# Edge counting in groups of 13 targets with keys fetched from device memory, and a re-ordered start, in a one-core graph layer

## The chip, the cores and the metric

The kernel runs on one core of a Trainium2 chip. The core has five engines with a queue each: TensorE (matmul; its weight loads are listed apart), VectorE, ScalarE, GpSimd and SyncE (which here only issues DMAs). They meet through semaphores, and 16 DMA engines serve all queues. The metric is the device time of one execution in microseconds, the median of the timed runs.

## The reference

One layer of a graph transformer over N = 1250 nodes with D = 1024 features, and 41250 edges (20000 random ones in both directions and a self loop for each node), sorted by target `dst`:

```python
xn = _layernorm(x)
# graph convolution: adds self loops once more, symmetric norm
deg  = segment_sum(ones, dst);  dinv = rsqrt(deg)
gnn  = relu(segment_sum((xn @ W)[src] * (dinv[src] * dinv[dst])[:, None], dst) + b)
# linear attention, 16 heads: phi(k) = elu(k) + 1
mix  = (phi(Q) @ (phi(K).T @ V)) / (phi(Q) @ sum(phi(K)) + 1e-6) @ Wo.T + bo
x = x + gnn + mix
# gated feed-forward with two gelu layers of 512, then back to 1024
x = x + ffn(_layernorm(x))
```

The message sum is done as a product with the 1250 x 1250 matrix of edge counts, so the kernel must count how many edges go from each source to each target.

## The kernel before, in words

Nodes are tiled by 128: NT = 10 tiles, the last of 98. Every float32 product is made of three float32r matmuls with high and low parts, so each weight slice of 128 x 512 needs a copy ("hi", `weight_hi`) and a remainder ("lo", `weight_lo`) before use. Remainders are made strictly in order of the slices, since each waits for the count `w_ready` of the one before; the list `LO_FIRST` says which of the first ten VectorE makes, GpSimd makes the others.

The first phase has 40 steps: 4 slabs of key and value weights by 10 node tiles. In a step TensorE makes 24 matmuls of 512 columns (`gemm_rows`), then the key-value sums of the step before (`kv_sum`). In steps 1 to 8 it first transposes the next node tile (`transpose_tile`), in step 0 the second tile within the product. A node tile goes this way: rows arrive in `xrow` (two buffers), VectorE takes the statistics (`ln_stats`), ScalarE the root (`ln_root`), VectorE finishes (`ln_finish`), ScalarE applies (`ln_apply`), TensorE transposes, ScalarE copies the high part (`transposed_hi`), VectorE makes the remainder (`transposed_lo`). VectorE takes the statistics of tile s + 3 in its step s, behind its work on the unit of that step (`kb`, `kmin`).

Edges are counted in the same steps. VectorE prepares keys, constants and chunk ranges in `edge_parts` of its steps 1 to 5 and 8, with an all-reduce on GpSimd between. A group ("window") is 16 targets of a tile. SyncE loads the group's first chunk number from `bounds` and copies 6 chunks of 128 keys from the key table in SBUF (`keys_load`); VectorE makes one-hots of sources and of (target, source tile) (`window`); TensorE multiplies them, 6 matmuls of 160 columns a group; ScalarE copies the counts out (`adj_out`); VectorE adds a finished tile up (`count_tile`). From step 10 on there are three groups a step, `windows_of`; TensorE does the groups of a step behind its product in the next step, two ahead of `kv_sum` and the rest behind. A group with more than 6 chunks would take a slower path under an `If`, which these inputs never enter.

Then follow queries, the graph product, its aggregation, the mixing and the feed-forward part, which the change does not touch. Engines are in-order queues and everything is placed by hand: what stands behind a wait on its engine waits too.

## Time and profile before

| | us |
|---|---|
| median of 3 runs (lowest to highest) | 1010.98 (1010.98 to 1013.32) |
| the profiled execution | 1012.45 |
| its span between first and last instruction | 1010.6 |
| TensorE busy | 986.4 (98%) |
| VectorE busy | 560.3 (55%) |
| ScalarE busy | 292.6 (29%) |
| GpSimd busy | 143.2 (14%) |
| mean granted clock of TensorE | 0.996 of 2.4 GHz |

The profiled execution lies between the lowest and the highest of the timed runs. Busy time of TensorE includes matmuls that overlap their neighbours, so costs are read as distances between starts. "L1444" is a line of the printed kernel.

### The profile page before, as it was taken

How to read it: one execution, taken by the hardware profiler on the slowest of the kernel's cores; microseconds unless marked ns; L12 is line 12 of the kernel's file. 1: busy time of each engine (PE TensorE's matmuls, PEld its weight loads, DVE VectorE, ACT ScalarE, POOL GpSimd, SP SyncE). 2: the span in 40 equal slices, each digit the busy share in tenths (PEclk: the TensorE clock that was granted, in tenths of full speed). 3: DMA queues.
4: the chain of work that ended last, by engine and by line, in shares of the span. 5: the costliest groups of instructions: out<-in, count | busy, mean ns of one | idle time of the engine just before them, and what ended most of it. 6: DMA issues, size and time to landing. Idle time of an engine off the chain costs nothing.

```text
span 1010.6 us, 13193 instructions
## 1 busy us (share of the span) xinstructions
PE 986.4 (98%) x4932; PEld 835.3 (83%) x4932; DVE 560.3 (55%) x1033; ACT 292.6 (29%) x564; POOL 143.2 (14%) x192
## 2 busy tenths in 40 slices
PE   4999999999999999999999999999999999999998
PEld 3878888888889988978787688767778999999986
DVE  5886768778754788893112465446655412122354
ACT  5783213214114243241212222113213212135300
POOL 7011001001002023050300000000300203055100
PEclk9999999999999999999999999999999999999999
DMA  7313103013002003122020566445421402010053
GB/s 279 116 50 97 30 17 111 18 32 98 15 28 85 26 26 134 50 70 93 21 86 15 161 190 190 139 146 167 162 88 54 167 1 84 1 42 1 21 186 138
DMA packets 44077, 86.74 MB, mean 86 GB/s; under 512 B 16152, under 2 KB 20612, under 8 KB 43992
## 3 DMA queue, kind: packets, MB, share of 16 engines
q1 hardware_dynamic: 35512, 57.20, 17.3%
q0 software_dynamic: 8480, 28.45, 8.8%
q8 instruction: 48, 0.79, 0.3%
q14 instruction: 37, 0.30, 0.1%
HBM read 61.38 MB, written 23.76 MB: 84 GB/s over the span
## 4 chain that ended last, share of the span: by engine, by line
PE 90%; DVE 6%; ACT 1%; issue 1%; POOL 1%; DMA 1%; DVEq 0%; ACTq 0%; POOLq 0%
PE PS L1405 10%; PE PS L1407 10%; PE PS L1406 10%; PE PS L1511 9%; PE PS L1512 9%; PE PS L1513 9%; PE PS L1569 5%; PE PS L1571 4%; PE PS L1444 3%; PE PS L1588 3%; PE PS L1589 3%; PE PS L1590 3%; PE PS L1640 2%; PE PS L1642 2%; PE PS L1641 2%; PE PS L1420 2%
## 5 line engine op out<-in xcount | busy, mean ns | idle before, releaser
L1405 PE MATMUL PS<-ring,act_t 128*128 128x512 f32 (+1 forms) x480 | 194.6, 405 | 1.7 <-DVE act_t L967 0.9
L1407 PE MATMUL PS<-ring,act_t 128*128 128x512 f32 (+1 forms) x480 | 190.7, 397 | 0.0
L1406 PE MATMUL PS<-ring,act_t 128*128 128x512 f32 (+1 forms) x480 | 190.2, 396 | 0.0
L1511 PE MATMUL PS<-act_t,ring 128*128 128x416 f32 (+1 forms) x432 | 159.3, 369 | 1.4 <-POOL ring L423 1.3
L1512 PE MATMUL PS<-act_t,ring 128*128 128x416 f32 (+1 forms) x432 | 152.1, 352 | 0.0
L1513 PE MATMUL PS<-act_t,ring 128*128 128x416 f32 (+1 forms) x432 | 151.8, 351 | 0.0
L1405 PEld LDWEIGHTS PS<-ring,act_t 128*128 128x128 f32 (+1 forms) x480 | 89.9, 187 | 23.9 <-POOL ring L423 1.6
L1407 PEld LDWEIGHTS PS<-ring,act_t 128*128 128x128 f32 (+1 forms) x480 | 89.5, 186 | 22.4
L1406 PEld LDWEIGHTS PS<-ring,act_t 128*128 128x128 f32 (+1 forms) x480 | 89.8, 187 | 21.4 <-issue 0.5
L1511 PEld LDWEIGHTS PS<-act_t,ring 128*128 128x128 f32 x432 | 81.3, 188 | 6.8 <-issue 3.4
L1512 PEld LDWEIGHTS PS<-act_t,ring 128*128 128x128 f32 x432 | 81.4, 188 | 4.1 <-issue 3.4
L1513 PEld LDWEIGHTS PS<-act_t,ring 128*128 128x128 f32 x432 | 81.2, 188 | 0.9
L1190 DVE RECIPROCAL rec<-rec 128x416 f32<-128x416 f32 (+1 forms) x24 | 65.9, 2746 | 0.0
L722 ACT ACTIVATE ctile<-PS 128x160 uint16<-128x160 f32 x80 | 23.2, 300 | 137.2 <-PE PS L1444 136.3
L604 POOL DMA_DIRECT2D stage_x<-in_wslices_dram x54 | 29.3, 547 | 207.5 <-DVE ring L423 203.7
L1056 DVE TENSOR_TENSOR oh_dst<-iota,kcur 128x960 bf16<-128x960 int16 x80 | 52.0, 650 | 0.0
L1340 DVE SCALAR_TENSOR_TENSOR hb<-PS,scl,sil 128x416 f32<-128x416 f32 (+1 forms) x12 | 7.8, 651 | 75.3 <-PE PS L1513 75.3
L1125 DVE TENSOR_TENSOR kb<-PS,kvb 128x256 f32<-128x256 f32 (+1 forms) x40 | 16.9, 424 | 52.6 <-issue 38.3
L423 POOL TENSOR_TENSOR ring<-stage,ring 128x512 fp32r<-128x512 f32 x23 | 31.0, 1348 | 99.9 <-ACT ring L728 97.7
L1055 DVE TENSOR_TENSOR oh_src<-iota,kcur 128x768 bf16<-128x768 int16 x80 | 44.1, 551 | 0.3
L423 POOL TENSOR_TENSOR ring<-stage_x,ring 128x512 fp32r<-128x512 f32 x28 | 38.2, 1364 | 38.0 <-ACT ring L728 26.9
L1444 PE MATMUL PS<-oh_dst,oh_src 128*128 128x160 bf16 x480 | 43.2, 233 | 0.0
(185 smaller groups left out, 1654.1 us busy)
## 6 DMA issues: line engine op xcount, KB each, us to landing
stage_x<-in_wslices_dram POOLq DMA_DIRECT2D x54, 256.0 KB, 4.2
stage<-in_wslices_dram POOLq DMA_DIRECT2D x42, 256.0 KB, 3.6
xr<-x_d SPq DMA_DIRECT2D x18, 512.0 KB, 3.4
phin_d<-phiq SPq DMA_DIRECT2D x8, 625.0 KB, 3.2
xrow<-in_x_dram SPq DMA_DIRECT2D x9, 512.0 KB, 3.7
xh<-in_x_dram SPq DMA_DIRECT2D x18, 256.0 KB
x_d<-xh SPq DMA_DIRECT2D x18, 256.0 KB
x_d<-xr SPq DMA_DIRECT2D x9, 512.0 KB, 2.7
```

What stands on the lines that cost most here:

```text
L423: eng.tensor_tensor(ring[:, slot(k), 1, :], stage_buf(n), ring[:, slot(k), 0, :].bitcast(F32), ALU.subtract).then_inc(w_ready, 1)
L1055: dve.tensor_tensor(oh_src[:, b], count(P), pairs(kcur[:, dt % 2, j, 0], P), ALU.is_equal)
L1056: dve.tensor_tensor(oh_dst[:, b], count(WCOLS), pairs(kcur[:, dt % 2, j, 1], WCOLS), ALU.is_equal).then_inc(onehot, 1)
L1190: dve.reciprocal(rec[:, i % 2, 0:n], rec[:, i % 2, 0:n]).then_inc(rec_ready, 1)
L1405: pe.matmul(out_ap, node_rows(0, k, t), ring[:, slot(k0 + k), 0, :], start=(k == 0), stop=False)
L1406: pe.matmul(out_ap, node_rows(1, k, t), ring[:, slot(k0 + k), 0, :], start=False, stop=False)
L1407: ins = pe.matmul(out_ap, node_rows(0, k, t), ring[:, slot(k0 + k), 1, :], start=False, stop=(k == KD - 1))
L1444: ins = pe.matmul(PS[:, b, 0:WCOLS], oh_src[:, o, j // 2, :, j % 2], oh_dst[:, o, j // 2, :, j % 2], start=(j == 0), stop=(j == STATIC_CHU ...
L1511: pe.matmul(out_ap, w[0], x_t[:, 0, k, o:o + n], start=(k == 0), stop=False)
L1512: pe.matmul(out_ap, w[0], x_t[:, 1, k, o:o + n], start=False, stop=False)
L1513: ins = pe.matmul(out_ap, w[1], x_t[:, 0, k, o:o + n], start=False, stop=(k == nk - 1))
L1569: pe.matmul(out_ap, lhs, h_rows(half, 0, st), start=(st == 0), stop=False)
```

## The change

It groups 13 targets (the last group of a tile has 11) in place of 16, 10 groups a tile and 100 in all, with 4 chunks of 128 edges each. The edges are laid out by rows (328 consecutive edges a partition) in place of columns. The key table is stored to device memory (`keys_d`), and each group's 512 keys are fetched from there, starting at any edge and not only at a multiple of 128. The first edge of every group is found by comparing with row bounds and by four small matmuls in TensorE's steps 4 and 6; GpSimd's all-reduce is gone. The fallback now counts all edges for a tile if any group has more than 512 edges or the edges are unsorted. There are four groups a step in steps 10 to 34, and five one-hot buffers in place of three.

At the start the first tile's rows come in two halves of 512 columns with a semaphore each, and the first norm is applied in halves ahead of all weight copies. VectorE makes the remainders of slices 0, 1, 3, 5 and 7, with the third tile's statistics ahead of the last. The root and finish of the third tile stand ahead of step 0. The third tile's rows go to `st_blk` (a buffer used much later) and are requested when the fourth weight slice is in, ahead of the edges; GpSimd clears `st_blk` afterwards. The second tile's transposes stand two slices later in the first product.

```diff
@@ constants @@
-STATIC_CHUNKS = 6
+STATIC_CHUNKS = 4
+CAPACITY = STATIC_CHUNKS * P
-OH_BUFS = 3
+OH_BUFS = 5
-WIN = 16
+WIN = 13
-LO_FIRST = (3, 5, 7)
+LO_FIRST = (0, 1, 3, 5, 7)
@@ windows_of @@
-    if 10 <= step < 37:
-        return list(range(3 * (step - 10), min(3 * (step - 9), NWIN)))
+    if 10 <= step < 35:
+        return list(range(4 * (step - 10), 4 * (step - 9)))
@@ block.sync @@
-            sp.dma_start(xrow[:, 0, :], xrows(x, 0)).then_inc(x_in[0], 16)
-            sp.dma_start(xrow[:, 1, :], xrows(x, 1)).then_inc(x_in[1], 16)
-            sp.dma_start(e_src[:], src_cols).then_inc(edges_in, 16)
-            sp.dma_start(e_dst[:], dst_cols).then_inc(edges_in, 16)
-            sp.dma_start(d_rows[0:ROWS_P], dst_rows).then_inc(edges_in, 16)
+            for g in range(2):
+                sp.dma_start(xrow[:, 0, 512 * g:512 * g + 512], x[0:P, 512 * g:512 * g + 512]).then_inc(x_first[g], 16)
+            sp.dma_start(x_tile(1), xrows(x, 1)).then_inc(x_in[1], 16)
+            sp.wait_ge(stage_in[stage_slot(3)], 16)
+            sp.dma_start(x_tile(2), xrows(x, 2)).then_inc(x_in[2], 16)
+            sp.dma_start(e_src[:], src_rows).then_inc(edges_in, 16)
+            sp.dma_start(e_dst[:], dst_rows).then_inc(edges_in, 16)
...
-            for t in range(2, NT):
-                sp.wait_ge(xn_ready, t - 1)
-                sp.dma_start(xrow[0:rows(t), t % 2, :], xrows(x, t)).then_inc(x_in[t % 2], 16)
+            for t in range(3, NT):
+                sp.wait_ge(xn_ready, t - 1 if t > 4 else t - 2)
+                sp.dma_start(x_tile(t), xrows(x, t)).then_inc(x_in[x_buf(t)], 16)
+                if t == 3:
+                    sp.wait_ge(keys_ready, 1)
+                    sp.dma_start(keys_d.rearrange("(p c) k -> p (c k)", p=P),
+                                 keys[:, 0:ROWL].rearrange("p c k -> p (c k)")).then_inc(keys_stored, 16)
...
-                    first = sp.value_load(bounds[0:1, w:w + 1], min_val=0, max_val=NCH)
-                    sp.dma_start(kraw[:, dt % KEY_BUFS, j], keys[:, bass.ds(first, STATIC_CHUNKS), :]).then_inc(keys_got[dt], 16)
+                    first = sp.value_load(bounds[0:1, w:w + 1], min_val=0, max_val=LAST_FIRST)
+                    sp.dma_start(kraw[:, dt % KEY_BUFS, j],
+                                 keys_d[bass.ds(first, CAPACITY), :].rearrange("(p c) k -> p c k", p=P)).then_inc(keys_got[dt], 16)
@@ block.gpsimd @@
-            pool.wait_ge(score_ready, 1)
-            nc.gpsimd.partition_all_reduce(sall[:], smax[:], P, RMAX).then_inc(bounds_max, 1)
+            pool.wait_ge(xn_ready, 3)
+            nc.gpsimd.memset(st_blk[:], 0.0).then_inc(consts, 1)
@@ block.vector @@
-            def edge_ranges():
...
+            def edge_rows():
+
+                link(dve.tensor_copy(d_row[:, 0:ROWL + 1], e_dst[:]))
+                link(dve.tensor_copy(first_d[:], d_row[:, 0:1]))
+                link(dve.memset(first_d[0:1], -1.0))
+                link(dve.tensor_scalar(row_of[:], thr[:], first_d[:], None, ALU.is_gt))
+                dve.scalar_tensor_tensor(row_of[:], thr[:], d_row[:, ROWL:ROWL + 1], row_of[:], ALU.is_le,
+                                         ALU.mult).then_inc(rows_known, 1)
+
+            def edge_order():
+                link(dve.tensor_tensor(below[:], d_row[:, 0:ROWL], d_row[:, 1:ROWL + 1], ALU.is_gt))
+                link(dve.tensor_reduce(unsorted[:], below[:], AX.X, ALU.max))
...
+            edge_parts = {1: edge_keys, 2: edge_constants, 3: edge_rows, 4: edge_order, 5: edge_starts, 7: edge_bounds}
@@ block.tensor @@
-                    ins = pe.matmul(PS[:, b, 0:WCOLS], oh_src[:, o, j // 2, :, j % 2], oh_dst[:, o, j // 2, :, j % 2],
+                    n = width(w) * NT
+                    ins = pe.matmul(PS[:, b, 0:n], oh_src[:, o, j // 2, :, j % 2], oh_dst[:, o, j // 2, 0:n, j % 2],
...
+            def group_rows():
+                a = slice(0, NWIN + 1)
+                pe.wait_ge(rows_known, 1)
+                pe.matmul(PS[a, 7, 0:ROW_COLS], row_of[:], d_row[:], start=True, stop=True)
+                pe.matmul(PS[a, 7, THR_COL:THR_COL + 1], thr[0:1], ones[0:1, 0:1], start=True, stop=True).then_inc(rows_got, 1)
```

Three places show how instructions moved. The first is SyncE's queue at its beginning, before: rows of node tiles go to `xrow`, those of tiles 2 to 9 by the eight loads of L445; `d_rows` are the targets for the ranges.

```order
L434 DMA xrow<-in_x_dram 128x1024
L435 DMA xrow<-in_x_dram 128x1024
L436 DMA e_src<-in_src_cols_dram 128x336
L437 DMA e_dst<-in_dst_cols_dram 128x336
L438 DMA d_rows<-in_dst_rows_dram 108x384
L440 DMA kvb<-in_bkv_dram 128x512 x2
L441 DMA bq_sb<-in_bq_dram 128x8
L442 DMA scl<-in_scales_dram 128x16
L445 DMA xrow<-in_x_dram 128x1024 x7
```

And with the change, where `st_blk` holds the third tile's rows and `keys_d` is the key table in device memory:

```order
L464 DMA xrow<-in_x_dram 128x512 x2
L465 DMA xrow<-in_x_dram 128x1024
L467 DMA st_blk<-in_x_dram 128x1024
L468 DMA e_src<-in_src_rows_dram 128x328
L469 DMA e_dst<-in_dst_rows_dram 128x329
L471 DMA kvb<-in_bkv_dram 128x512 x2
L472 DMA bq_sb<-in_bq_dram 128x8
L473 DMA scl<-in_scales_dram 128x16
L476 DMA xrow<-in_x_dram 128x1024
L479 DMA keys_d<-keys 128x656
L476 DMA xrow<-in_x_dram 128x1024 x5
```

The third tile moved ahead of the edges, and the store of the keys stands between the loads of the fourth and the fifth tile.

The second is ScalarE from its first root to the tenth weight copy, before (`ring` is written by weight copies, `xn` by the norm, `act_t` by the high part of a transposed tile, `ln` by the root):

```order
L690 ACTIVATE ln<-ln 128x1
L728 ACTIVATE ring<-stage 128x512 x2
L704 ACTIVATE xn<-xrow,ln 128x1024
L728 ACTIVATE ring<-stage 128x512 x2
L711 ACTIVATE act_t<-PS 128x4x128 x2
L690 ACTIVATE ln<-ln 128x1
L728 ACTIVATE ring<-stage_x 128x512 x2
L704 ACTIVATE xn<-xrow,ln 128x1024
L728 ACTIVATE ring<-stage_x 128x512 x4
```

And with the change:

```order
L724 ACTIVATE ln<-ln 128x1
L739 ACTIVATE xn<-xrow,ln 128x512
L742 ACTIVATE xn<-xrow,ln 128x512
L767 ACTIVATE ring<-stage 128x512
L724 ACTIVATE ln<-ln 128x1
L749 ACTIVATE act_t<-PS 128x4x128 x2
L767 ACTIVATE ring<-stage 128x512 x3
L767 ACTIVATE ring<-stage_x 128x512
L742 ACTIVATE xn<-xrow,ln 128x1024
L767 ACTIVATE ring<-stage_x 128x512 x5
L724 ACTIVATE ln<-ln 128x1
L749 ACTIVATE act_t<-PS 128x4x128 x2
```

The norm of the first tile stands in halves ahead of the copies, two of the roots stand ahead of the step loop's work, and each tile's high part comes earlier among the copies.

The third is TensorE in a counting step, from the end of its product to the branch of the fallback, before:

```order
L1406 MATMUL PS<-ring,act_t 128x512
L1407 MATMUL PS<-ring,act_t 128x512
L1405 MATMUL PS<-ring,act_t 128x512
L1406 MATMUL PS<-ring,act_t 128x512
L1407 MATMUL PS<-ring,act_t 128x512
L1444 MATMUL PS<-oh_dst,oh_src 128x160 x12
L1420 MATMUL PS<-phik,vt 128x128 x2
L1444 MATMUL PS<-oh_dst,oh_src 128x160 x6
L1450 COMPARE_AND_BRANCH
```

And with the change:

```order
L1441 MATMUL PS<-ring,act_t 128x512
L1439 MATMUL PS<-ring,act_t 128x512
L1440 MATMUL PS<-ring,act_t 128x512
L1441 MATMUL PS<-ring,act_t 128x512
L1479 MATMUL PS<-oh_dst,oh_src 128x130 x8
L1454 MATMUL PS<-phik,vt 128x128 x2
L1479 MATMUL PS<-oh_dst,oh_src 128x130 x8
L1485 COMPARE_AND_BRANCH
```

Eighteen matmuls of 160 columns became sixteen of 130, four groups in two pairs around the key-value sums.

## Rows read from the trace of the kernel before

**Rows 1.** The page: span, then busy us, share and instructions of each engine

```profile
span 1010.6 us, 13193 instructions
...
PE 986.4 (98%) x4932; PEld 835.3 (83%) x4932; DVE 560.3 (55%) x1033; ACT 292.6 (29%) x564; POOL 143.2 (14%) x192
```

**Rows 2.** Waits of TensorE: who waited, for whom, us in total, times, longest

```profile
PE PS L1387 <- ACT xn L704: 16.2, 5, 9.5
```

**Rows 3.** Timeline: start us, us, engine line op out<-in xcount [idle before]

```profile
4.45 1.42 DVE L937 BATCH_NORM_STATS2 stats<-xrow 128x6 f32<-128x512 f32 x2 [4.45 <-DMA xrow<-in_x_dram]
...
8.15 1.23 ACT L704 ACTIVATE xn<-xrow,ln 128x1024 f32<-128x1024 f32 x1
...
9.52 1.94 PE L1387 MATMUL PS<-ident,xn 128*128 128x128 f32 x8 [9.52 <-ACT xn L704]
...
16.48 1.29 POOL L423 TENSOR_TENSOR ring<-stage_x,ring 128x512 fp32r<-128x512 f32 x1 [1.52 <-ACT ring L728]
...
17.88 0.69 DVE L423 TENSOR_TENSOR ring<-stage_x,ring 128x512 fp32r<-128x512 f32 x1 [2.12 <-POOL ring L423]
...
22.62 1.24 ACT L704 ACTIVATE xn<-xrow,ln 128x1024 f32<-128x1024 f32 x1 [2.06 <-DVE ln L960]
...
23.92 1.97 PE L1387 MATMUL PS<-ident,xn 128*128 128x128 f32 x8 [2.84 <-ACT xn L704]
```

**Rows 4.** The timeline of VectorE in its steps 1 to 4

```profile
30.84 0.51 DVE L979 SCALAR_TENSOR_TENSOR keys<-e_dst,e_hi 128x336 f32<-128x336 int32 x1
...
32.78 1.42 DVE L937 BATCH_NORM_STATS2 stats<-xrow 128x6 f32<-128x512 f32 x2
...
36.53 1.28 DVE L967 TENSOR_TENSOR act_t<-PS,act_t 128x512 fp32r<-128x512 f32 x2
...
45.02 0.19 DVE L992 MEMSET smax<- 128x160 f32 x1
...
47.93 0.42 DVE L1125 TENSOR_TENSOR kb<-PS,kvb 128x256 f32<-128x256 f32 x1
...
53.56 0.27 DVE L1006 TENSOR_SCALAR score<-thr,d_rng 108x80 f32<-108x80 f32 x1
...
56.18 0.42 DVE L1125 TENSOR_TENSOR kb<-PS,kvb 128x256 f32<-128x256 f32 x1
```

**Rows 5.** The timeline of TensorE, the transposes of three steps

```profile
32.29 1.04 PE L1387 MATMUL PS<-ident,xn 128*128 128x128 f32 x8
...
39.19 1.04 PE L1387 MATMUL PS<-ident,xn 128*128 128x128 f32 x8
...
68.99 1.04 PE L1387 MATMUL PS<-ident,xn 128*128 128x128 f32 x8
```

**Rows 6.** The timeline of TensorE, starts of two steps without counting

```profile
82.52 0.47 PE L1405 MATMUL PS<-ring,act_t 128*98 128x512 f32 x1
...
88.52 0.48 PE L1405 MATMUL PS<-ring,act_t 128*128 128x512 f32 x1
```

**Rows 7.** The timeline of TensorE, a step with counting

```profile
122.85 1.03 PE L1444 MATMUL PS<-oh_dst,oh_src 128*128 128x160 bf16 x12
123.72 0.65 PE L1420 MATMUL PS<-phik,vt 128*128 128x128 f32 x4
124.20 0.59 PE L1444 MATMUL PS<-oh_dst,oh_src 128*128 128x160 bf16 x6
...
130.25 1.03 PE L1444 MATMUL PS<-oh_dst,oh_src 128*128 128x160 bf16 x12
```

**Rows 8.** SyncE: the key loads in its timeline, and the row loads of L445

```profile
81.30 37.61 SPq L464 DMA_DIRECT2D kraw<-keys  x32
...
DMA to landing us min/median/max: 3.5/4.7/7.5
```

**Rows 9.** TensorE near 699 us: timeline, and a stretch with granted clock (PEclk)

```profile
699.37 0.90 PE L1387 MATMUL PS<-ident,xn 128*128 128x128 f32 x3 [2.02 <-ACT xn L704]
...
699.50:702.70 3.20, 3.20 (x12) 2.91 (x13) 2.91 (x7) 1.04 (x4) 0.00 (x0) 0.50 0.59 191
```

283 lines of the change are left out of this document (150 added, 133 removed).

## Prediction, made before the changed kernel had run

> **What bounds the kernel now.** I read the page first. TensorE is busy for 986.4 of 1010.6 us [rows 1], so what counts is the work on TensorE itself and the few places where it stands still. The waits of TensorE name one large item: transposes that wait for a normalised tile from ScalarE, 16.2 us in five waits, the longest 9.5 us [rows 2]. One of them, 2.02 us, ends at 699.37 us [rows 9]; the others lie in the first 62 us. So a change can gain in two ways: fewer matmul columns after 62 us, where TensorE hardly waits, and less standing still before.
>
> In the counting steps the timeline of TensorE shows what counting costs. A step without it takes 88.52 - 82.52 = 6.00 us [rows 6], one with three groups 130.25 - 122.85 = 7.40 us [rows 7]. The 18 matmuls of 160 columns cost 1.40 us a step: 12 of them take 123.72 - 122.85 = 0.87 us, 72.5 ns each, and 0.095 us is change-over. Nothing waits there, so what leaves these steps leaves the total.
>
> Before 62 us the chain is another. TensorE starts at 9.52 us behind statistics (4.45) and the application of the norm (8.15), and gets its third tile only at 23.92 us [rows 3]. After that VectorE sets the pace, since it carries the preparation of the edges beside the norms [rows 4]: a step with transposes takes TensorE 39.19 - 32.29 = 6.90 us when nothing waits, but the next four take 68.99 - 39.19 = 29.80 us [rows 5], 2.2 us more than four of these. From 68.99 us on TensorE is bound by itself.
>
> **Counting: 13 targets and 4 chunks.** Before, 80 groups by 6 matmuls of 160 columns: 26 steps by 1.40 plus a rest of two groups, 12 x 0.0725 = 0.87 us, 37.3 us in all. Now 100 groups by 4 matmuls, 16 in each of 25 steps, 130 columns each (110 in the last group of every tile). The price of a 130-column matmul is not in the trace. From above it is bounded by today's 72.5 ns; from below by taking 30 columns off at the slope of the large matmuls: 24 of 512 columns take the 6.00 us of a bare step [rows 6] less 124.20 - 123.72 = 0.48 us of key-value sums [rows 7], 230 ns each, so (230 - 72.5)/352 = 0.45 ns a column and 59.0 ns. One column a cycle at 2.4 GHz, the level granted here, takes off 12.5 ns and gives 60.0. I take 59.5 ns, near the lower end, since 160 columns already take little more than their own 66.7 ns. A step then pays 16 x 0.0595 + 0.095 = 1.05 us, 25 steps 26.2 us, less 0.3 us for the narrow groups: 25.9 to 26.0 us. **Counting saves 11.3 us** (5.9 us at the upper price).
>
> The Trainium skill (TensorE: Matmul & The Clock Gate, section Back-to-back issue gap) speaks against this: it gives some 81 ns for every pair of weight load and 128-column matmul in a sustained stream. This trace, with 72.5 ns for 160 columns, is already below it; by the page's figure 400 matmuls would cost 32.4 us and change-over, a gain of 2.5 us in place of 11.3.
>
> VectorE builds fewer elements for it: per step four pairs of one-hots with 512 and 520 elements against three with 768 and 960, so its load falls along with the step, and I cost it at nothing; TensorE's long step hides it. ScalarE copies out four results a step in place of three, two of them ahead of the exponential; each fits under the key-value sums that follow on TensorE. SyncE fetches the keys with one load a group, 1.2 us each by its timeline (37.61 us for 32) [rows 8]. The first ten must be there for VectorE's step 10 near 94 us. The boundaries, now without GpSimd's all-reduce and one step earlier, come near 75 us, so the fetch of the first tile is done near 89 us: hidden by 5 us. The largest group of these sorted inputs holds 486 edges against a capacity of 512, so the fallback path is not entered.
>
> **The start.** The first rows come in halves, so one of the two statistics (half of 1.42 us) runs before 4.45 us and the norm is ready 0.7 us sooner. The application now goes ahead of the weight copies and in halves, and the first transposes move from 9.52 to about 7.8 us. That alone gives little: the first unit still waits for its slices, whose remainders alternate between VectorE (0.69 us) and GpSimd (1.29 us) and whose eighth ends at 17.88 + 0.69 = 18.57 us [rows 3]. In the new order the first transposed tile reaches VectorE near 9.7 us, its remainder is done at 11.0 and that of the second slice at 11.7; three turns of GpSimd and two of VectorE later it is 17.0, the third tile's statistics run until 17.75, and the eighth remainder ends near 18.4. What helps is that statistics and root of the third tile now stand ahead of this eighth slice and its finish right behind, where before 1.9 us of statistics and 1.3 us of another tile's remainder lay between. With some 1.2 us for the finish (five short instructions) and 1.3 us for the application, the third tile's transposes move from 23.92 to about 20.95 us, **3.0 us sooner**, and VectorE's step 1 with them: the edge keys are ready at 28.35 in place of 30.84 + 0.51 = 31.35 us [rows 4].
>
> **A new wait takes this back.** SyncE's queue now holds, between the rows of the fourth and the fifth tile, the store of the key table, and this waits for the edge keys. The fifth tile's rows are thus asked for at 28.35 + 0.45 us (0.45 for issuing the store). Such a load takes 3.5 us at least [rows 8]; behind a store of 336 KB up to 0.9 us more. They land between 32.3 and 33.2 us, and VectorE's statistics of this tile, which follow the edge keys within a microsecond and began at 32.78 us before [rows 4], begin there. Behind them on VectorE stand the step's key sums, the next norm and the next remainder. So VectorE's step 2 begins between 0.5 us earlier and 0.4 us later than before, though all ahead of it is 3 us earlier.
>
> From there the side work shrinks: the ranges of step 3, 47.93 - 45.02 = 2.91 us, become five short instructions of 1.4 us, and the scores of step 4, 56.18 - 53.56 = 2.62 us, become two over 328 columns, 1.1 us (an instruction of 336 columns takes 0.51 us) [rows 4]. VectorE's steps are then about 7.1 us at most and no longer hold TensorE. The fifth tile's transposes start behind the chain that those statistics open: 36.53 - 32.78 = 3.75 us to the next remainder [rows 4] and 1.3 us for this, so at 37.85 us; four steps of 6.9 us follow, plus the new row matmul of 330 columns (330/128 x 0.24 = 0.62 us, where two of 128 columns take 0.48 us [rows 7]), one of 101 columns (0.19) and two of one column (0.2 each at most, by the same row): 66.6 to 66.9 us at the place that the trace of before has at 68.99 us [rows 5]. **The start gains 2.2 us** (1.8 to 2.8). From here TensorE is its own bound in both.
>
> **Sum.** The profiled execution took 1012.45 us, 1.85 more than its span. Minus 11.3 and 2.2 it is 998.95. Two of three timed runs gave 1010.98, 1.47 below the profiled one; on the median the forecast is 1010.98 - 13.5 = 997.5 us. The half-speed stretch at 699.5 us (clock 0.50 for 3.4 us behind a stand of 2 us [rows 9]) costs 1.7 us when it comes, and may come or stay away in either kernel; this is the width of the forecast, 995.5 to 999.5.
>
> **Rivals.**
> The pace of short matmuls does not follow their columns. For it: a weight load accompanies each. Against: 160 columns are near their column time. At 72.5 ns the gain is 5.9 + 2.2: 1002.9 us.
> The weight loads do not hide under shorter matmuls, and a pair costs more than today. Counting gains nothing when 400 matmuls and 2.4 us of change-over reach 37.3 us, at 87 ns; midway from 72.5, at 80 ns, it gains 37.3 - 32.0 - 2.4 = 2.9 us: 1010.98 - 2.9 - 2.2 = 1005.9 us. Against it: nothing in the counting step of before shows a load that sticks out. The page of the Trainium skill named above describes this case.
> The fifth tile's rows aren't late after all, for instance because the edge keys come much sooner than I count. Then the 3.0 us carry through and the shorter side work adds its own: transposes of the eighth tile near 63.7 us, a gain of 5.3, and 994.4 us.
> The fifth tile's rows are later still (the store takes its full 2 to 3 us ahead of them): the start gains nothing, 999.7 us and up to 1001.
> Slower: fetching keys from device memory in 32-byte pieces runs at another pace than 1.2 us a load. With up to 1.7 us nothing waits; with p us a load counting ends near 75 + 100 p + 5 us against 269 without waits, so from p = 2.03 it eats the whole gain, and at twice today's pace, 2.4 us, it gives 997.5 + 51 = 1048 us. Against it: the trace shows SyncE's own instructions filling the 1.2 us, not the transfer.
>
> **Chances.** Forecast as summed 0.62; short matmuls at today's price 0.12; start gain carried through 0.10; start gains nothing 0.08; weight loads that stick out 0.03; slow fetches or another wait in counting that makes it slower 0.05 (0.01 of it near no change). The range 994 to 1003 us holds the first, second and fourth and half of the third. A difference under 0.3% (3 us) can't be told from none. All cases but the last lie 5 us or more below the median: faster 0.94, within 0.3% 0.02, slower 0.04.
>
> **What would show it.** Counting: steps near 7.05 us from the twelfth on, twelve to sixteen matmuls with starts 58 to 61 ns apart, no idle time of TensorE ahead of them. Start: first transposes at 7.8 us, the third tile's near 21. The new wait: VectorE's statistics of the fifth tile idle for 3 to 4 us behind the load of rows, the place named as DMA. The transposes of the eighth tile near 66.8 us. I am wrong if VectorE doesn't wait there, if the counting matmuls stay above 70 ns apart, or if one-hot building waits for keys.

## The result, and the profile after

| | before | changed |
|---|---|---|
| median of 6 runs each, us | 1012.67 | 1007.33 |
| lowest to highest | 1010.98 to 1016.65 | 1004.61 to 1007.82 |
| profiled execution | 1012.45 | 1007.65 |
| its span | 1010.6 | 1005.8 |
| TensorE busy | 986.4 | 980.2 |

The ratio is 0.9938, with a 95% interval of 0.9916 to 0.9961. The kernel is faster by 5.3 us in the medians (6.3 by the ratio); 13.5 us were forecast, and 1007.33 lies outside the range of 994 to 1003 us. (Of the 9.8 us between 997.5 and 1007.33, 1.7 are the median of before, which was 1010.98 when the forecast was made; 8.1 are the change.) The forecast calls the place at 68.99 us "the eighth tile"; counted from the first, these are the ninth tile's transposes, and so they are called here.

The page of the changed kernel, its lines that answer to [rows 1]:

```profile
span 1005.8 us, 13325 instructions
...
PE 980.2 (97%) x4860; PEld 827.2 (82%) x4860; DVE 545.5 (54%) x1069; ACT 293.9 (29%) x585; POOL 139.8 (14%) x189
```

TensorE's waits in it (who, for whom, us in total, times, longest) answer to [rows 2]:

```profile
PE PS L1421 <- ACT xn L739: 8.2, 1, 8.2
PE PS L1421 <- ACT xn L742: 5.6, 3, 2.2
PE PS L1439 <- DVE act_t L1004: 2.6, 1, 2.6
PE PS L1454 <- DVE phik L1170: 1.8, 1, 1.8
```

The 16.2 us of before are now 13.8 on the two lines of the norm, but 2.6 and 1.8 us stand beside them (the one for `act_t` was 0.9 us before), and one wait is new: that for `phik`. It stands in the middle of the start, as TensorE's timeline shows, to be held against [rows 3, 5]:

```profile
8.20 1.94 PE L1421 MATMUL PS<-ident,xn 128*128 128x128 f32 x8 [8.20 <-ACT xn L739]
...
23.20 0.97 PE L1421 MATMUL PS<-ident,xn 128*128 128x128 f32 x7 [1.39 <-ACT xn L742]
...
30.40 1.08 PE L1421 MATMUL PS<-ident,xn 128*128 128x128 f32 x8
...
38.86 0.71 PE L1454 MATMUL PS<-phik,vt 128*128 128x128 f32 x4 [1.81 <-DVE phik L1170]
41.80 1.96 PE L1421 MATMUL PS<-ident,xn 128*128 128x128 f32 x8 [2.22 <-ACT xn L742]
```

(The line at 23.20 us is cut off by its window; all eight transposes take 1.08 us.) Up to the fourth tile (30.40 us, 32.29 before) the change leads by 1.9 us. Part of that is clock: before, TensorE runs at half its clock from 23.56 us on for 3.4 us, which [rows 3, 5] show in eight transposes that take 1.97 us at 23.92 and 1.04 us later; with the change it doesn't there. The fifth tile's transposes start at 41.80, where before they start at 39.19. Behind them TensorE runs at half its clock (columns: stretch, length, then busy us of TensorE, weight loads, VectorE, ScalarE and GpSimd, the granted clock, DMA share, GB/s):

```profile
40.50:47.30 6.80, 5.50 (x17) 4.76 (x18) 6.28 (x20) 5.67 (x8) 0.00 (x0) 0.51 0.25 77
```

The place that [rows 5] have at 68.99 us comes at 73.55 us. So the start loses 4.6 us. It was forecast to gain 2.2. From the first counting matmul to the first product of the queries it is 208.8 us before (100.65 to 309.48) and 199.6 now (105.22 to 304.79): 9.3 us gained. Behind that the two kernels take the same (701 us). 9.3 - 4.6 = 4.7, against 4.8 between the spans: nothing is left to explain elsewhere.

The chain that ended last names what made the fifth tile late (start us, us, what):

```profile
31.26 0.51 DVE keys L1016
31.79 0.34 SPq L479
32.13 0.04 issue
32.17 4.42 DMA xrow<-in_x_dram
36.62 0.71 DVE stats L974
...
40.24 0.23 DVE ln L997
40.49 1.25 ACT xn L742
41.74 0.06 issue
41.80 1.96 PE PS L1421 x8
```

Edge keys, then SyncE's store of them (L479), then the load that stands behind it in SyncE's queue, then the statistics, norm and transposes: the new wait of the forecast, in its place. VectorE idles for it:

```profile
36.62 1.42 DVE L974 BATCH_NORM_STATS2 stats<-xrow 128x6 f32<-128x512 f32 x2 [4.08 <-DMA xrow<-in_x_dram]
```

### The profile page after: what moved, and what is told of

Its sections match the earlier page's. It is cut to its first block, busy times and chain, and to the rows that moved or that the text cites. A ratio compares the mean times of both kernels' runs of the same rounds, so it can differ in the third digit from the quotient of the medians.

```text
span 1005.8 us, 13325 instructions
## 1 busy us (share of the span) xinstructions
PE 980.2 (97%) x4860; PEld 827.2 (82%) x4860; DVE 545.5 (54%) x1069; ACT 293.9 (29%) x585; POOL 139.8 (14%) x189
## 4 chain that ended last, share of the span: by engine, by line
PE 91%; DVE 5%; DMA 1%; ACT 1%; issue 1%; POOL 1%; SPq 0%; DVEq 0%; ACTq 0%; POOLq 0%
PE PS L1439 11%; PE PS L1441 10%; PE PS L1440 10%; PE PS L1561 9%; PE PS L1560 9%; PE PS L1562 9%; PE PS L1618 5%; PE PS L1620 4%; PE PS L1638 3%; PE PS L1639 3%; PE PS L1637 3%; PE PS L1479 2%; PE PS L1454 2%; PE PS L1691 2%; PE PS L1690 2%; PE PS L1689 2%
## 5 line engine op out<-in xcount | busy, mean ns | idle before, releaser
L761 ACT ACTIVATE ctile<-PS 128x130 uint16<-128x130 f32 x100 | 23.7, 283 | 115.0 <-PE PS L1479 115.0
L640 POOL DMA_DIRECT2D stage<-in_wslices_dram x42 | 23.0, 550 | 182.5 <-DVE ring L440 179.9
L440 POOL TENSOR_TENSOR ring<-stage,ring 128x512 fp32r<-128x512 f32 x21 | 28.5, 1355 | 106.2 <-ACT ring L767 104.4
L1086 DVE TENSOR_TENSOR oh_dst<-iota,kcur 128x520 bf16<-128x520 int16 x100 | 42.2, 422 | 0.0
L1085 DVE TENSOR_TENSOR oh_src<-iota,kcur 128x512 bf16<-128x512 int16 x100 | 41.9, 419 | 0.3
```

The lines of the kernel that those rows point to most:

```text
L440: eng.tensor_tensor(ring[:, slot(k), 1, :], stage_buf(n), ring[:, slot(k), 0, :].bitcast(F32), ALU.subtract).then_inc(w_ready, 1)
L640: pool.dma_start(stage_buf(n), wslices[n]).then_inc(stage_in[stage_slot(n)], 16)
L1085: dve.tensor_tensor(oh_src[:, b], count(P), pairs(kcur[:, dt % 2, j, 0], P), ALU.is_equal)
L1086: dve.tensor_tensor(oh_dst[:, b], count(WCOLS), pairs(kcur[:, dt % 2, j, 1], WCOLS), ALU.is_equal).then_inc(onehot, 1)
```

## The experiments

All times are medians; "ratio" is to the kernel before on the same chip, with its 95% interval. The last two columns are the starts of the fifth and ninth tile's transposes in the profiled execution. e1 to e4 ran side by side, so did e5 to e8, e9 to e12, and e13 with e14; medians compare best within such a group.

| kernel | us | ratio | 5th | 9th |
|---|---|---|---|---|
| before | 1012.67 | | 39.19 | 68.99 |
| changed | 1007.33 | 0.9938 [0.9916, 0.9961] | 41.80 | 73.55 |
| e10, changed again | 1007.01 | 0.9943 [0.9931, 0.9956] | 41.41 | 72.12 |
| e1, store behind the rows | 998.76 | 0.9864 [0.9836, 0.9892] | 37.35 | 66.81 |
| e12, e1 again | 1000.41 | 0.9878 [0.9863, 0.9893] | 37.45 | 66.91 |
| e4, before with the store | 1016.62 | 1.0038 [1.0024, 1.0053] | 41.78 | 72.88 |
| e9, changed, stands filled | 1005.74 | 0.9934 [0.9922, 0.9947] | 42.22 | 71.67 |
| e8, old start, new counting | 1003.31 | 0.9906 [0.9886, 0.9926] | 40.33 | 69.41 |
| e2, e1 and late slices | 998.66 | 0.9866 [0.9838, 0.9895] | 36.71 | 65.95 |
| e3, e1 and whole first rows | 999.53 | 0.9871 [0.9843, 0.9900] | 36.60 | 66.06 |
| e7, e1, e2 and e3 | 998.49 | 0.9862 [0.9841, 0.9883] | 35.77 | 65.23 |
| e11, e7 with the store in place | 1003.91 | 0.9916 [0.9902, 0.9931] | 39.49 | 70.20 |
| e13, e2 and late clearing | 999.16 | 0.9864 [0.9839, 0.9889] | 37.22 | 66.31 |
| e14, e7 and late clearing | 999.07 | 0.9859 [0.9836, 0.9882] | 35.61 | 64.92 |
| e5, e1 without the fallback | 999.60 | 0.9871 [0.9849, 0.9892] | 35.52 | 64.98 |
| e6, e1 with half the columns | 994.37 | 0.9818 [0.9798, 0.9838] | 36.67 | 66.12 |

### Is it the place of the store? e1, e4, e10, e12

e1 moves the store behind all row loads:

```diff
             for t in range(3, NT):
                 sp.wait_ge(xn_ready, t - 1 if t > 4 else t - 2)
                 sp.dma_start(x_tile(t), xrows(x, t)).then_inc(x_in[x_buf(t)], 16)
-                if t == 3:
-                    sp.wait_ge(keys_ready, 1)
-                    sp.dma_start(keys_d.rearrange(...), keys[...]).then_inc(keys_stored, 16)
+            sp.wait_ge(keys_ready, 1)
+            sp.dma_start(keys_d.rearrange(...), keys[...]).then_inc(keys_stored, 16)
```

> One edit to the changed kernel: the store of the key table leaves its place between the row loads of the fourth and the fifth tile and stands behind all row loads. Theory A (the store's wait for the edge keys delays the fifth tile's rows, and the stand of TensorE that follows brings the half-speed stretch at 40.5 us): VectorE's wait of 4.1 us at 36.6 us is gone, the fifth tile's transposes (41.80 us in the changed kernel) start at 37.5 to 38, no half-speed stretch follows them, the ninth... tile of transposes that stood at 73.55 us starts at 66 to 67.5, and the median falls from 1007.3 to about 1000.5 us. Rival B (VectorE's own steps of 7.1 us set the pace anyway): the wait goes, but only some 3 us come back, about 1004 us. Rival C (the rows are late for another reason): no change.

e4 is the reverse: the kernel before, with a store of its key table ahead of the fifth tile's load. Its only other addition is a wait for this store ahead of the key loads, which start at 85.6 us, long after it.

```diff
             for t in range(2, NT):
                 sp.wait_ge(xn_ready, t - 1)
+                if t == 4:
+                    sp.wait_ge(keys_ready, 1)
+                    sp.dma_start(keys_d, keys[:].rearrange("p c k -> p (c k)")).then_inc(keys_stored, 16)
                 sp.dma_start(xrow[0:rows(t), t % 2, :], xrows(x, t)).then_inc(x_in[t % 2], 16)
```

> The kernel before, with one thing added: a store of its key table to device memory that waits for the edge keys and stands in SyncE's queue ahead of the fifth tile's rows. Nothing reads it. Theory A (that place in the queue costs by itself): the rows are requested at 31.8 us in place of 24.0, the statistics of the fifth tile start near 36.2 us (32.78 before), the fifth tile's transposes near 42.5 (39.19 before), and the median rises by 3 to 4.5 us over the kernel before. Rival B (the long VectorE steps 3 and 4 absorb it): less than 1.5 us more.

Both went the way of the store. In e1 VectorE goes from its first piece of step 1's unit straight into the statistics:

```profile
31.97 0.29 DVE L1157 TENSOR_SCALAR kmin<-kb 128x256 f32<-128x256 f32 x1
32.17 1.42 DVE L973 BATCH_NORM_STATS2 stats<-xrow 128x6 f32<-128x512 f32 x2
```

In e4, whose edge keys are ready when those of before are, it stands:

```profile
32.69 0.29 DVE L1132 TENSOR_SCALAR kmin<-kb 128x256 f32<-128x256 f32 x1
36.60 1.42 DVE L943 BATCH_NORM_STATS2 stats<-xrow 128x6 f32<-128x512 f32 x2 [3.62 <-DMA xrow<-in_x_dram]
```

One store of 336 KB, read by nobody, makes the kernel before 4.1 us slower than its median of 1012.5 beside it. e10 and e12 then put the changed kernel and e1 on one chip:

> The changed kernel itself, unchanged, beside e12 on one chip, so that the price of the key store's place stands in one comparison. Theory (the store in SyncE's queue costs the late rows and the half-speed stretch behind them): 8 to 8.6 us more than e12, ratio to before 0.994. Rival (part of the 8.6 us between the first measurement of the changed kernel and e1 was a difference of chips): 4 to 6 us more than e12.

> The kernel of e1 again (key store behind all row loads), beside the changed kernel on one chip. Theory: ratio to before 0.9865, 8 to 8.6 us under the changed kernel. Rival: 4 to 6 us under it.

They are 6.6 us apart (1007.01 and 1000.41), between the two expectations: some of the 8.6 us between the first two medians (7.5 us by their ratios) was not the store. Part of it is the clock late in the kernel: three of e1's four timed runs had a mean clock of 1.000 and took 997.8 to 998.9 us, the fourth had 0.998 and took 1000.7; three of e12's four had 0.998 (1000.3 to 1001.1 us), one 1.000 (999.5). At the ninth tile the traces put the price at 6.7 us (73.55 and 66.81) and 5.2 us (72.12 and 66.91). So the store's place costs 6.6 to 8.6 us in the medians, of which 5.2 to 6.7 stand where it acts; either is about the whole gain of the change as it was made (5.3 us), or more.

### How much of it is the clock? e9

```diff
+            def filler(n):
+                for _ in range(n):
+                    pe.matmul(PS[:, 7, :], node_rows(0, 0, 0), ring[:, slot(KV0), 0, :], start=True, stop=True)
...
+                if step == 3:
+                    filler(9)
                 if 1 <= step < 9:
                     transpose_tile(step + 1)
...
+                if step == 2:
+                    filler(7)
                 if step >= 1:
                     kv_sum(step - 1)
```

> The changed kernel, with the store in its place, and 16 additional matmuls of 512 columns on TensorE in the two stands before the fifth tile's transposes (7 ahead of the key-value sums of step 1, which waited 1.81 us, 9 ahead of the transposes, which waited 2.22 us); their results are overwritten and used nowhere. At 0.23 us each they fill 1.6 and 2.1 us and take nothing from other work. Question: how much of the changed kernel's loss at the ninth tile (73.55 us against 66.8 in e1) is the late rows themselves and how much the half-speed stretch of 6.8 us from 40.5 us on that follows the stand. Theory: the stretch follows TensorE's standing still, and is about half of its length in lost time; filled, the clock stays at 1.0 there, the fifth tile's transposes stay at 41.8 us, the ninth's move from 73.55 to 70.6 us, and the time falls by 3 us, ratio 0.991. Rival: the stretch doesn't hang on the stand, the clock still falls near 40 us, the ninth tile stays at 73.5 us, ratio 0.994.

The filler is L1514 of TensorE's timeline:

```profile
36.80 1.80 PE L1514 MATMUL PS<-ring,act_t 128*128 128x512 f32 x7
39.28 0.71 PE L1454 MATMUL PS<-phik,vt 128*128 128x128 f32 x4 [0.69 <-DVE phik L1170]
39.75 2.34 PE L1514 MATMUL PS<-ring,act_t 128*128 128x512 f32 x9
42.22 1.09 PE L1421 MATMUL PS<-ident,xn 128*128 128x128 f32 x8
```

and the same stretch as above now reads

```profile
40.50:47.30 6.80, 6.67 (x33) 5.26 (x32) 6.32 (x20) 5.43 (x8) 0.00 (x0) 1.00 0.25 77
```

The clock holds, although the rows are as late as ever. From the fifth to the ninth tile it takes 71.67 - 42.22 = 29.45 us, as in e1 (66.81 - 37.35 = 29.46), and 31.75 in the changed kernel: the half-speed stretch costs 2.3 us there. In e10 it was shorter:

```profile
41.90:45.30 3.40, 3.40 (x13) 2.83 (x12) 3.12 (x11) 2.47 (x4) 0.00 (x0) 0.51 0.45 154
```

and cost 72.12 - 41.41 - 29.45 = 1.3 us. The median of e9 is 1.3 us below e10, not the 3 us expected: the stretch is not always the long one, and the filler itself pushed the fifth tile back by 0.4 to 0.8 us. The intervals of the two ratios overlap, so the medians alone don't show it; the mean clocks of the timed runs do: 0.998 to 1.000 in all six of e9, 0.995 or 0.996 in all six of e10. So that the stretch follows the stands is shown; its price is 1.3 to 2.3 us, and the larger part of the loss is the late rows themselves (41.80 against 37.35 us at the fifth tile, 4.45 us).

### Why were the edge keys late? e2, e3, e11, e13

The forecast had the edge keys ready at 28.35 us. The chain shows 31.26 + 0.51. Two causes show in VectorE's timeline of the changed kernel:

```profile
9.43 0.69 DVE L974 BATCH_NORM_STATS2 stats<-xrow 128x6 f32<-128x512 f32 x1 [2.22 <-DMA xrow<-in_x_dram]
...
23.41 1.20 DVE L1158 TENSOR_SCALAR kmin<-kb 128x256 f32<-128x256 f32 x1
...
26.28 1.25 DVE L1170 SCALAR_TENSOR_TENSOR phik<-kb,kexp 128x256 f32<-128x256 f32 x1
```

against these of before:

```profile
7.65 1.41 DVE L937 BATCH_NORM_STATS2 stats<-xrow 128x6 f32<-128x512 f32 x2
...
22.95 0.43 DVE L1126 TENSOR_SCALAR kmin<-kb 128x256 f32<-128x256 f32 x1
...
25.63 0.43 DVE L1138 SCALAR_TENSOR_TENSOR phik<-kb,kexp 128x256 f32<-128x256 f32 x1 [0.49 <-ACT kexp L758]
```

The second tile's statistics wait 2.22 us for their rows, and two instructions take 0.8 us more each. e3 loads the first tile's rows at once again (VectorE then waits for them once, which the cut below leaves out); e2 lets GpSimd make its remainders 9 and 10 later:

```diff
-            for g in range(2):
-                sp.dma_start(xrow[:, 0, 512 * g:512 * g + 512], x[0:P, 512 * g:512 * g + 512]).then_inc(x_first[g], 16)
+            sp.dma_start(xrow[:, 0, :], xrows(x, 0)).then_inc(x_first[0], 16)
```

> The edit of e1, and the first tile's rows come in one load as in the kernel before, not in halves. Theory A (the halves with their packets of 2048 bytes are why the second tile's rows landed at 9.4 us, where they landed at 5.7 before): the second tile's statistics start at 6 to 7.5 us, the first statistics at 4.45, and the third tile's transposes (23.20 us in the changed kernel) start at 21 to 22. Rival B (the rows are late because they share the DMA engines with the slices, whatever the packets): the second statistics stay at 9 to 9.5 us and the transposes at 23 to 24.

```diff
             nc.gpsimd.memset(st_blk[:], 0.0).then_inc(consts, 1)
+            pool.wait_ge(xn_ready, 8)
             for n in range(8, 42):
```

> The edit of e1, and GpSimd makes the remainders of the ninth and tenth slice only after the eighth norm has been applied (in the changed kernel it makes the ninth from 25.90 us on, beside VectorE's step 0). Theory A (two short VectorE instructions of step 0, kmin at 23.41 us and phik at 26.28 us, take 1.20 and 1.25 us in place of 0.43 because GpSimd works at that time): phik is back at 0.43 us, VectorE's step 1 begins 0.8 us sooner than in e1, and the median is 0.8 us lower. Rival B (they are long for another reason, or the time is hidden): no difference from e1 within 0.3 us at the transposes.

In e3 the second tile's statistics start at 7.56 us, right behind the first tile's work:

```profile
7.56 1.41 DVE L972 BATCH_NORM_STATS2 stats<-xrow 128x6 f32<-128x512 f32 x2
```

The stretch from 4 to 5 us shows what differs. With the halves (2,048 bytes a row) under way, the DMA engines moved 201 GB/s in the changed kernel, and 389 in e3 (last column):

```profile
4.00:5.00 1.00, 0.00 (x0) 0.00 (x0) 0.97 (x2) 0.00 (x0) 1.00 (x3) 1.00 0.78 201
```

```profile
4.00:5.00 1.00, 0.00 (x0) 0.00 (x0) 0.64 (x1) 0.00 (x0) 1.00 (x3) 1.00 0.97 389
```

All profiled executions together: with whole first rows (before, e3, e4, e7, e8, e11, e14) the second tile's statistics start between 7.51 and 7.72 us and never wait, and that microsecond has 385 to 430 GB/s. With halves they start at 9.43 (changed), 9.14 (e1, e2), 9.17 (e12), 9.28 (e9), 8.99 (e10), 9.63 (e13), 7.98 (e6) and 7.07 us (e5), and the microsecond has 176 to 377 GB/s. So the halves bring the statistics of the first half forward by 0.4 to 1 us (3.93 in the changed kernel, 3.37 to 3.49 elsewhere, 4.36 in e3), and the second tile's arrival scatters, mostly 1.5 to 2 us late. Which property of the halves does it isn't shown: their rows are half as long, and the second tile's rows are also requested behind two loads, at 1.67 us in place of 1.21. This scatter also lies under the table: e5 and e12 have the same start as e1, and e5's fifth tile is 1.8 us sooner by it. Differences under 2 us between kernels with halves aren't read from that column alone.

In e2 `phik` is back:

```profile
25.98 0.41 DVE L1170 SCALAR_TENSOR_TENSOR phik<-kb,kexp 128x256 f32<-128x256 f32 x1
```

and `kmin` stays at 1.21. e13 also takes GpSimd's clearing of `st_blk` away from there:

```diff
-            nc.gpsimd.memset(st_blk[:], 0.0).then_inc(consts, 1)
             pool.wait_ge(xn_ready, 8)
+            nc.gpsimd.memset(st_blk[:], 0.0).then_inc(consts, 1)
```

> The base is e2 (key store behind all row loads, GpSimd's ninth and tenth remainder late). GpSimd now also clears st_blk only behind the eighth norm. Theory: kmin of the first step is held by this clearing and falls from 1.21 to 0.43 us, phik stays at 0.41, and VectorE's work of step 1 starts 0.5 to 0.8 us sooner than e2's 27.83 us. Rival: GpSimd's issuing of the eight weight loads ahead of the clearing holds it; then kmin stays at 1.2 us. The total time in either case within 1 us of e2, ratio 0.9855 to 0.987.

```profile
23.62 0.29 DVE L1158 TENSOR_SCALAR kmin<-kb 128x256 f32<-128x256 f32 x1
...
25.59 0.41 DVE L1170 SCALAR_TENSOR_TENSOR phik<-kb,kexp 128x256 f32<-128x256 f32 x1
```

Both instructions are held while GpSimd works, one by its remainder, one by its clearing, and the change had put both under VectorE's longest chain. The Trainium skill (SBUF — State Buffer, section SBUF: two separate sides) describes a port pair that VectorE and GpSimd share and that one of them holds for a whole instruction; 1.21, 1.21 and 0.29 us for the same `kmin` in e1, e2 and e13 agree with it: the difference of 0.92 us is nearly the 1.01 us that the clearing takes. The recorded start of the clearing (24.68 us in e2) lies 0.4 us behind the end of `kmin`, so the trace alone would not have named it; e13 does.

Step 1 of VectorE started at 27.83 us in e2 and at 28.02 in e13, but e13's whole start ran 0.5 us later (third tile at 23.39, 22.88 in e2); from the third tile on it is 4.63 us against 4.95, half of what was expected. TensorE makes nothing of it: from the third to the fifth tile's transposes it takes 13.83 us in both.

The two causes don't make up all of the 3.4 us. The edge keys are ready at 31.77 us in the changed kernel, 31.47 in e1, 30.72 in e3, 30.62 in e2, 29.89 in e7 (both edits) and 29.56 in e14 (late clearing as well): with both causes undone they are still 1.2 us behind the 28.35 us of the forecast. 0.8 us of this is there already at the third tile (21.78 us against 20.95), whose forecast counted on the halves; the rest has no experiment.

Is this time worth anything? Where the row load waits for the edge keys, it is. e11 has e2's and e3's edits with the store where the change put it:

> The changed kernel, the store in its place, but with the first rows in one load (as e3) and GpSimd's ninth and tenth remainder late (as e2). The question is whether a quicker VectorE, worth nothing in e7 where no row load waits for the edge keys, is worth something where one does. Theory: the edge keys, and so the store and the fifth tile's rows, come 1.5 us sooner: VectorE's statistics of that tile at 35.1 in place of 36.62 us, its transposes at 40.3 in place of 41.80, the ninth's at 72.0 in place of 73.55, ratio 0.9925. Rival: the rows' landing is set by the transfers ahead of them and not by the request, and nothing moves: 0.994.

Its store goes out at 29.87 in place of 31.79 us, the statistics start at 34.31 in place of 36.62, and it is 3.1 us faster than the changed kernel on the same chip (e10). At the ninth tile 1.9 us of these show (70.20 and 72.12); its profiled execution also lacks the half-speed stretch that e10's has at 694 us.

```profile
34.31 1.42 DVE L974 BATCH_NORM_STATS2 stats<-xrow 128x6 f32<-128x512 f32 x2 [3.68 <-DMA xrow<-in_x_dram]
```

### Is it worth anything once the store is out of the way? e7, e14

> The base is e1, with e2's wait (GpSimd makes the remainders of slices 9 and 10 only behind the eighth norm) and e3's first rows in one load. Each alone brought the transposes 0.7 to 0.9 us forward, e2 by freeing two instructions of VectorE that stood still beside GpSimd, e3 by letting the second tile's rows land sooner. Theory: the two lie one behind the other on VectorE before the edge keys, so the sum holds: the fifth tile's transposes at 36.0 us (37.35 in e1), the ninth's at 65.2 (66.8 in e1), and the time 1.6 us below e1, ratio 0.985. Rival: what comes forward on VectorE is given back where TensorE sets the pace by itself, and the time is e1's, ratio 0.9865.

> The base is e7 (e1, e2 and e3 together), with the clearing of st_blk late as in e13. Theory: each piece of VectorE's time before the edge keys passes on to the transposes, so the fifth tile's come at 35.0 to 35.3 us (35.77 in e7) and the ninth's at 64.5 (65.23), and the time falls by 0.7 us to a ratio of 0.9855. Rival: from some point TensorE is its own bound in the start, the fifth tile's transposes stay near 35.8 us, and the ratio is e7's 0.986.

In the transposes the pieces add up in e7 (35.77 and 65.23 us, 1.6 before e1) and all but stop in e14: 35.61 - 21.78 = 13.83 us from the third to the fifth tile is two steps of 6.9, TensorE's own time. That is the rival of e14. In the medians neither shows: 998.49 and 999.07, against 998.76 and 1000.41 for e1 and its repetition. Ratios of 0.9859 to 0.9878 with half intervals of 0.0015 to 0.003 can't separate 1.6 us. The fastest version is one of this family, some 12 to 14 us under the kernel before; which one is open.

### What is the re-ordered start worth? e8

e8 has the new counting, the store behind the rows, and the start of before: whole first rows, third tile's rows in `xrow` behind the edges, weight copies ahead of the first norm, remainders 3, 5 and 7 on VectorE. It also has e2's late remainders, so its nearest kin is e7, on the same chip.

```diff
-LO_FIRST = (0, 1, 3, 5, 7)
+LO_FIRST = (3, 5, 7)
...
-            sp.wait_ge(stage_in[stage_slot(3)], 16)
-            sp.dma_start(x_tile(2), xrows(x, 2)).then_inc(x_in[2], 16)
...
+            hi(1)
             ln_apply(0)
+            hi(2)
+            hi(3)
...
+            ln_root(1)
+            hi(4)
+            hi(5)
...
+                if step == 0:
+                    ln_root(2)
```

> It has the counting and the edge preparation of the change, with the key store behind all row loads as in e1, but the start of the kernel before: the first rows in one load, the third tile's rows behind the edges in its old buffer, weight copies ahead of the first norm, remainders of slices 3, 5 and 7 on VectorE, root and finish of the third tile in the first step, GpSimd's ninth and tenth remainder late. Theory: the re-ordered start is worth what the transposes show against the kernel before: the third tile's 23.92 us before and 22.90 in e1, so about 1 us, while the step that carries the edge keys sets the next; the fifth tile's transposes at 38.5 us (37.35 in e1), the ninth's at 68.0 (66.81 in e1), ratio 0.9875. Rival 1: the re-ordered start brings nothing once the store is out of the way, since VectorE has the same work before the edge keys; times as e1, ratio 0.9865. Rival 2: it loses (its halves hold up the second tile's rows and two VectorE instructions stand still beside GpSimd), and the old start is faster: 66.0 at the ninth tile, ratio 0.9855.

1003.31 us: the re-ordered start is worth 4.8 us against e7, more than the 1 us of the first theory and against both rivals. In the profiled executions e8 is 2.1 us behind e7 at the third tile and 4.2 at the ninth (69.41 and 65.23). Where it comes from shows at the third tile:

```profile
23.88 1.97 PE L1416 MATMUL PS<-ident,xn 128*128 128x128 f32 x8 [3.35 <-ACT xn L734]
```

```profile
22.40:29.20 6.80, 5.32 (x17) 4.55 (x18) 5.52 (x16) 6.25 (x9) 1.50 (x3) 0.52 0.75 284
```

TensorE stands for 3.35 us ahead of the third tile, and within this stand the clock halves for 6.8 us. With the old order it halves in every profiled execution: beside a stand of 2.84 us before (from 23.56 us on) and of 2.30 us in e4 (from 24.99 us on), for 3.4 us each. In the thirteen with the new order the stand is 1.06 to 1.40 us and the clock holds. So part of what the new order saves is a stand short enough for the clock to hold, and that is in no sum of instruction times.

### What sets the price of a counting matmul? e5, e6

e5 leaves out the branch with the fallback count on TensorE and VectorE; e6 lets the second to fourth chunk of a group multiply 65 columns in place of 130:

```diff
-                    n = width(w) * NT
+                    n = width(w) * NT if j == 0 else 5 * width(w)
```

> The base is e1 (the changed kernel with the key store behind all row loads). It leaves out the fallback count of TensorE and VectorE, which these inputs never enter, with its branch; all else is as in e1. The question is why counting saved 9.3 us in the changed kernel (from the first counting matmul to the queries 208.8 us before, 199.6 after) where 11.3 were forecast. Theory: the matmuls' price was right (60.8 ns measured against 59.5), and the rest went to the branch, which now stands apart from the degree matmul and comes once a tile: such a step took 7.28 us and one without it 7.10, so 10 x 0.18 us. Then the stretch falls from 199.6 us in e1 to 197.8, and the time by 1.6 to 1.8 us against e1, to a ratio of about 0.985 to the kernel before. Rival: the change-over between groups costs more than counted in every step and the branch costs nothing; then every step stays at its 7.1 to 7.28 us, the stretch at 199.6, the ratio at e1's 0.986 to 0.987.

> The base is e1. The second, third and fourth chunk of each group multiply only the columns of the first five source tiles, 65 in place of 130 (55 in place of 110), so the edges of those chunks whose sources lie in the last five tiles aren't counted: 300 of 400 matmuls are half as wide. The question is what sets the 60.8 ns between short matmuls. Theory A, their columns: 65 fewer at one a cycle of 2.4 GHz take off 27 ns, spacing 34 ns for three of four, 300 x 0.027 = 8.1 us less than e1, ratio about 0.978. Theory B, the weight load beside each (128 columns, by its own 53 ns at one column a cycle) is the floor: spacing 53 to 60 ns, 0.3 to 2.1 us less than e1, ratio 0.985 to 0.987. The Trainium skill (TensorE: Matmul & The Clock Gate, section Back-to-back issue gap) would have some 81 ns for every pair with 128 columns, and the changed kernel already shows 60.8 ns for 130.

The steps of TensorE read as follows, in the changed kernel

```profile
105.22 0.66 PE L1479 MATMUL PS<-oh_dst,oh_src 128*128 128x130 bf16 x8
105.72 0.66 PE L1454 MATMUL PS<-phik,vt 128*128 128x128 f32 x4
106.22 0.65 PE L1479 MATMUL PS<-oh_dst,oh_src 128*128 128x130 bf16 x8
...
112.33 0.65 PE L1479 MATMUL PS<-oh_dst,oh_src 128*128 128x130 bf16 x8
```

and in e6 (the rows name the widest of the eight, 130 columns; six of them have 65)

```profile
104.63 0.48 PE L1478 MATMUL PS<-oh_dst,oh_src 128*128 128x130 bf16 x8
104.95 0.69 PE L1453 MATMUL PS<-phik,vt 128*128 128x128 f32 x4
105.47 0.48 PE L1478 MATMUL PS<-oh_dst,oh_src 128*128 128x130 bf16 x8
...
111.44 0.47 PE L1478 MATMUL PS<-oh_dst,oh_src 128*128 128x130 bf16 x8
```

The starts of the 400 matmuls lie 60.8 ns apart on average in the changed kernel (72.4 ns for the 480 of 160 columns before), and behind the 65-column ones of e6 the next starts after 33 ns on average. The price follows the columns, down to half of what the change uses. The Trainium skill (TensorE: Matmul & The Clock Gate, section Back-to-back issue gap) gives some 81 ns for a weight load with a 128-column matmul; this trace does not agree: even 160 columns take 72.4 ns here, and the measurement decides. The stretch from counting to queries falls by 5.6 us in e6 (199.6 in e1, 194.0), of 8.1 expected: part of the saved time comes back as gaps behind the groups (up to 0.29 us). The largest stand in the steps with the fallback's branch, most of which get only 0.12 to 0.18 us shorter than in e1, where most of the others get 0.25 to 0.29; why is open.

In e5 the same stretch is 198.7 us, 0.9 less than in e1 and not 1.8. That is clear of noise in the traces: in the twelve executions that have this counting unchanged it is 199.4 to 199.6 us. Its steps take 7.03 to 7.11 us except those with degree matmuls (7.30 to 7.32) and two of 7.75. The medians can't resolve it (999.60 us is no less than e1). So the branch costs 0.9 us in the changed kernel. Before, it stood in one step with the degree matmul, and such a step took 0.19 to 0.23 us more than others; now a step with the degree matmul alone takes as much, so beside it the branch had cost next to nothing.

## Why the prediction was wrong

**Counting: mechanism right, size off by 2.0 us.** The price taken, 59.5 ns, measured 60.8, and the first rivals (72.5 ns, 80 ns) are out. Against 11.3 us the stretch gave 9.3. The terms that were mis-sized are the price (400 x 1.3 ns = 0.5 us), the fallback's branch, which has no term because these inputs never enter it (0.9 us, e5), and change-over, the remaining 0.6 us: a plain step takes 7.07 to 7.11 us where 7.05 stood. No one-hot waited for keys: the first 40 loads of `kraw` take 44.36 us, 1.1 us each, and no instruction of VectorE waits for one.

**The start: the step that failed is "3.0 us sooner", the edge keys at 28.35 us, on which the price of the new wait was built.** The third tile came at 23.20 in place of 20.95 us, and the keys were 0.4 us later than before and not 3.0 sooner. Forecast for the ninth tile was 66.8 us; it came at 73.55. By the forecast's own chain:
- The edge keys, forecast for 28.35, are ready at 31.77: 3.4 us. The halves made the second tile's rows late (e3, and the scatter above), and two VectorE instructions were held by GpSimd's work (e2, e13). Undoing both brings 2.2 us (e14); 1.2 us stay without a tested cause. I had counted what the moved instructions take and not what they stand beside.
- The rows' landing after the request: 4.45 us, just beyond the upper end of 3.5 to 4.4, where 3.98 was used; with 0.1 us more from the statistics to the transposes this makes 0.55.
- From the fifth to the ninth tile: 31.75 us against 28.95. 2.3 of it is the half-speed stretch (e9), the rest steps of 7.2 and 7.9 us where 6.9 and 7.7 were counted. The forecast priced such a stretch only near 699 us, as width.

3.4 + 0.55 + 2.8 = 6.75 us, the whole of the difference; with the 2.0 us of counting it is the 8.75 us between the forecast's span (1010.6 - 13.5 = 997.1 us) and the measured 1005.85.

**"A new wait takes this back": right in place and kind, wrong in its price.** The forecast had it eat the 3 us which the start gained. Its price is 6.6 to 8.6 us (e12, e1), since it is counted from where VectorE and TensorE would be without it. I read the store as a delay of one load; it ties the fifth tile's rows to the last result of a chain, so every later slip of this chain (3.4 us here) goes on to TensorE, as e11 shows from the other side: its store goes out 1.9 us sooner, and its fifth tile's transposes start 2.3 us sooner than in the changed kernel, 1.9 sooner than in e10. The rival "rows later still" named this and stopped at 1001 us, because it let the start lose no more than its gain. A start slower than before was in none of the cases, and so not in the range. None of the three signs of being wrong that it names came: VectorE waited there (4.08 us), the counting matmuls are under 70 ns apart, and no one-hot waited for keys. It was wrong all the same, in sizes.

**The rival "rows not late" was e1.** It gave 994.4 us; e1 gave 998.76 and 1000.41. Its ninth tile is at 66.8 in place of 63.7 us, and counting lacks 2.0 us. That 66.8 us is also what was forecast for the changed kernel is chance: there a third tile 3.0 us sooner and a wait were to cancel in part, and e1 has no such wait and a third tile only 1.0 us sooner (22.90 us). Its span is 11.7 us under the one before, of which 2.2 come from the start and 9.2 from counting.

**The half-speed stretch near 699 us**, priced at 1.7 us, came in the profiled executions of before, the changed kernel, e1, e3, e8, e10 and e14 (688 to 699 us) and stayed away in e2, e5, e6, e7, e9, e11, e12 and e13; e12 has one at 369 us instead, e4 two, at 670 and 708. Two of six timed runs of the changed kernel show a higher mean clock (0.998 in place of 0.995) and are some 2.5 us shorter; which stretch they lack can't be told without a trace. The stand of 2.0 us ahead of that place is in executions with the stretch (e1) and without it (e5, e7, e12), so what lets it come in one and not in the next is open. The forecast also left out the half-speed stretch that the kernel before has in its start, at 23.56 us.

## What to carry to other kernels

An instruction that waits on an in-order DMA queue lends its lateness to everything requested behind it. Before a store of a computed table goes between two loads, ask which result it waits for and how far ahead of the consumers that result is; when it isn't far, put the store behind the last load that matters. One such line was worth more here (6.6 us on one chip) than the re-ordered start (4.8) and less than the re-grouped counting (9.3).

And when work is moved, price it where it lands: a split load slowed the load behind it, and GpSimd work that came to lie beside VectorE's chain lengthened instructions that nobody had touched.

## What the runs showed of the hardware that I had not expected

- Two loads of 2,048 bytes a row in place of one of 4,096: 176 to 377 GB/s against 385 to 430 between 4 and 5 us, and the consumer of the next load starts between 7.07 and 9.63 us in nine executions, in place of 7.51 to 7.72 in seven.
- A VectorE instruction of 0.29 us took 1.21 us beside GpSimd's clearing of a buffer, and one of 0.41 us took 1.25 us beside GpSimd's remainder.
- A 65-column matmul with its own weight load every 33 ns, where 130 columns take 60.8 and 160 take 72.4 ns.
- Two stands of TensorE shortly after each other (1.81 and 2.22 us in one execution, 1.79 and 2.23 in another) went with a granted clock of 0.51 for 6.8 and 3.4 us; 16 useless matmuls in their place kept the clock at 1.00. A single stand of 2.30 to 3.35 us at the third tile went with half clock in three executions, one of 1.06 to 1.40 us in none of thirteen.
